# The first batch's keys of the first cross attention, made in the side attention's stage instead of ahead of the main attention

## The reference, cut to what matters

```python
y_dca = y[:, -DCA:, :]                    # the 16 side rows
y_main = y[:, :-DCA, :]                   # 1585 rows
kv_dca = (y_dca @ Wkv_dca + bkv_dca).reshape(b, DCA, 2, H, HD)
k_dca = _ln(kv_dca[:, :, 0], kn_dca_w, kn_dca_b)
v_dca = kv_dca[:, :, 1]
q = _ln((x @ Wq + bq).reshape(b, s1, H, HD), qn_w, qn_b)
kv = jnp.concatenate([y_main @ Wk + bk, y_main @ Wv + bv], axis=-1)
k = _ln(kv.reshape(b, s2, H, 2 * HD)[..., :HD], kn_w, kn_b)
ctx = _attn(qT, k.transpose(0, 2, 1, 3), v.transpose(0, 2, 1, 3))
ctx_dca = _attn(qT, k_dca.transpose(0, 2, 1, 3), v_dca.transpose(0, 2, 1, 3))
return (ctx + DCA_WEIGHT * ctx_dca) @ Wo + bo
```

## Time and profile before

| | us |
|---|---|
| median of 3 runs | 2436.7 |
| lowest, highest | 2436.36, 2438.23 |
| the profiled execution | 2434.61 |
| its span | 2432.8 |
| span to the first scores of the main attention | 120.72 |

### The profile page before, as it was taken

One profiled execution on the slowest core, in us unless ns is written; L12 is line 12 of the kernel. 1 busy time (PEld: TensorE's weight loads), 2 busy tenths in 40 slices (PEclk: granted clock), 3 DMA queues, 4 the chain that ended last, 5 costly groups with the idle time before them and its releaser, 6 DMA issues. The chain is left out here.

```text
span 2432.8 us, 47536 instructions
## 1 busy us (share of the span) xinstructions
PE 2227.4 (92%) x16972; PEld 1759.8 (72%) x16972; DVE 1589.0 (65%) x2655; ACT 1179.8 (48%) x2263; POOL 1031.2 (42%) x709
## 2 busy tenths in 40 slices
PE   4699999999998999979999999999999999788866
PEld 2677777777775888857777788888888887666644
DVE  5368877888787333334532788888888885566673
ACT  2355656665653333313213676676766673333241
POOL 5159888988895000001110455455455461111320
PEclk8699999999999999979999999999999999899989
DMA  3000000001001222114212000000000001211200
GB/s 117 0 28 28 29 29 2 29 29 42 10 2 37 66 69 69 39 24 100 69 66 66 28 28 10 21 28 18 12 28 28 1 27 44 67 40 44 87 1 18
DMA packets 106429, 89.92 MB, mean 37 GB/s; under 512 B 33105, under 2 KB 86625, under 8 KB 106225
## 3 DMA queue, kind: packets, MB, share of 16 engines
q1 hardware_dynamic: 105936, 87.21, 12.0%
q0 software_dynamic: 288, 0.00, 0.0%
HBM read 86.15 MB, written 1.05 MB: 36 GB/s over the span
## 5 line engine op out<-in xcount | busy, mean ns | idle before, releaser
L2508 POOL TENSOR_TENSOR xT<-xT,x1b_ring 128x512 f32<-128x512 f32 (+1 forms) x176 | 248.4, 1411 | 210.4 <-ACT x1b_ring L2665 203.5
L1096 POOL TENSOR_TENSOR x0b_krstd<-x0b_krstd,minus_half 128x24 f32<-128x24 f32 x64 | 266.8, 4169 | 85.9 <-DVE x0b_krstd L1163 83.1
L1116 POOL TENSOR_TENSOR xT<-xT,x0b_ring 128x512 f32<-128x512 f32 (+1 forms) x167 | 233.1, 1396 | 31.5 <-ACT x0b_ring L1351 15.6
L111 DVE TENSOR_TENSOR x1b_plo<-x1b_ring,x1b_phi 128x512 fp32r<-128x512 f32 (+1 forms) x208 | 224.1, 1078 | 6.0 <-issue 4.9
L1351 ACT ACTIVATE x0b_ring<-x0b_ring 128x512 f32<-128x512 f32 (+1 forms) x208 | 131.0, 631 | 168.3 <-DVE x0b_ring L1181 160.7
L2680 ACT ACTIVATE x1b_ring<-x_ps,x1b_keymask 128x512 f32<-128x512 f32 (+1 forms) x208 | 142.9, 687 | 130.3 <-DVE xT L2587 125.5
L116 PE MATMUL x_ps<-x1b_qy,x1b_yT 128*128 128x512 f32 (+1 forms) x416 | 175.1, 421 | 4.7 <-ACT x1b_ring L2680 3.3
L1194 DVE TENSOR_TENSOR x0b_ring<-x_ps,x0b_krstd 128x512 f32<-128x512 f32 (+1 forms) x208 | 142.6, 685 | 56.0 <-PE x_ps L956 54.0
L2587 DVE SCALAR_TENSOR_TENSOR xT<-x_ps,x1b_keymask,xT 128x512 f32<-128x512 f32 (+1 forms) x176 | 131.3, 746 | 57.6 <-PE x_ps L118 56.4
L116 PE MATMUL x_ps<-x1b_phi,x1b_yv 128*128 128x512 f32 (+1 forms) x416 | 166.3, 400 | 0.8 <-ACT x1b_out_sb L2647 0.8
L118 PE MATMUL x_ps<-x1b_qy,x1b_yT 128*128 128x512 f32 (+1 forms) x416 | 163.8, 394 | 0.0
(11 more groups left out here) (610 smaller groups left out, 5665.6 us busy)
## 6 DMA issues: line engine op xcount, KB each, us to landing
x_y<-in_ctx_dram SPq DMA_DIRECT2D x8, 1536.0 KB
x_y<-in_ctx_dram SPq DMA_DIRECT2D x24, 512.0 KB, 3.9
a_wn<-in_L_attn_W_Q_dram SPq DMA_DIRECT2D x16, 256.0 KB, 3.1
a_wn<-in_L_attn_W_K_dram SPq DMA_DIRECT2D x16, 256.0 KB, 3.6
a_wn<-in_L_attn_W_V_dram SPq DMA_DIRECT2D x16, 256.0 KB, 4.3
a_won<-in_L_attn_W_O_dram SPq DMA_DIRECT2D x16, 256.0 KB, 2.9
x1a_wq<-in_L_xattn_Wq_dram SPq DMA_DIRECT2D x8, 512.0 KB, 9.0
x_y<-in_L_xattn_Wo_dram SPq DMA_DIRECT2D x8, 512.0 KB, 3.6
```

The lines of the kernel that those rows point to most:

```text
L111: return v.tensor_tensor(lo, exact, hi.bitcast(F32), ALU.subtract)
L1096: ins = g_.tensor_tensor(r, r, c.minus_half[:, 0:8].unsqueeze(1).broadcast_to([P, whole, 8]), ALU.pow)
L1116: g_.tensor_tensor(total[half][0:m, :], old, src, ALU.add).then_inc(summed, 1)
L2508: g_.tensor_tensor(total[half][0:m, :], old, src, ALU.add).then_inc(summed, 1)
```

## The change

What the preparation and the 19 opening entries of the first batch need (tiles, semaphores, the entry code, the lists HERE and AHEAD) is now a class `Keys` in the outer stage, and all of it runs in x0a. There the entries have two PSUM banks, 4 and 5; the side attention's scores move to banks 2 and 3, and the side values are projected into bank 6 behind the last transposes of the heads. A list `PLAN`, read by all four engines, lays the groups' steps (S scores, F probabilities, O outputs) among the entries (X, so many of the list). The placing of the side values on ACT is split in four, one quarter behind each exponential, and PE waits for it in front of the first O rather than of the first S. The first queries are placed at the very end of x0a's ACT stream. In x0b the main attention begins with step 0. The steps and their entries are unchanged.

```diff
+class Keys:
+    OPEN_BANKS = (4, 5)
+    def put(self, name, banks):
+        bank = banks[self.number % len(banks)]
+        self.place[name] = bank, self.uses[bank]
+        self.uses[bank] += 1
+        self.number += 1
...
+    def make(self, pe, seq, e):
+        bank, nth = self.place[seq, e]
+        out = self.ps[:, bank, :]
+        pe.wait_ge(self.kv_free[bank], nth + 1)
...
+        PLAN = [("S", 0), ("X", 2), ("S", 1), ("F", 0), ("S", 2), ("X", 1), ("F", 1), ("S", 3), ("X", 1), ("F", 2), ("O", 0),
+                ("X", 2), ("F", 3), ("O", 1), ("X", 4), ("O", 2), ("O", 3), ("X", 9)]
...
             @block.vector
+                v.wait_ge(loaded_m, 24 * 16)
+                keys.vector_zero(v)
                 v.wait_ge(wv_done, 4)
...
-                for g in range(0, HG0, 2):
-                    for u in range(2):
-                        sm.vector_before_exp(v, ps[:, 4 + u, :], u, g + u)
-                    for u in range(2):
-                        sm.vector_after_exp(v, u, g + u)
+                for op, k in plan():
+                    if op == "S":
+                        sm.vector_before_exp(v, ps[:, 2 + k % 2, :], k % 2, k)
+                    if op == "F":
+                        sm.vector_after_exp(v, k % 2, k)
+                    if op == "X":
+                        keys.vector_take(v, 0, k)
...
             @block.tensor
+                def project_side_values():
+                    pe.wait_ge(bank_read, 3)
...
                 pe.wait_ge(scaled, T + 4)
-                pe.wait_ge(vs_done, 16)
-                scores(0)
-                scores(1)
...
+                keys.prepare(pe)
+                for op, k in plan():
+                    if op == "S":
+                        scores(k)
+                    if op == "F":
+                        flip(k)
+                    if op == "O":
+                        values(k)
+                    if op == "X":
+                        if k[0] == "K":
+                            pe.wait_ge(wkv_done, CC)
+                        keys.make(pe, 0, k)
...
             @block.scalar
+                for op, k in plan():
+                    if op == "S":
+                        sm.scalar_exp(act, k % 2, k)
+                        keep_side_values(k)
+                    if op == "F":
+                        tail(k)
+                    if op == "O":
+                        evacuate(k)
+                    if op == "X":
+                        keys.scalar_take(act, 0, k)
+                keys.place_queries(act, 0, 0)
...
-                steps(lambda e: make(0, e), step)
+                steps(step)
```

More of the change, by code:

```diff
@@ L525, in _ @@
                                       ).then_inc(wv_done, 1)
+                for op, k in plan():
+                    if op == "X" and k[0] == "T":
+                        keys.deviations(g, 0, k[1], k[2])
             @block.vector
@@ L643, in _ @@
                     flip_heads(j)
+                project_side_values()
                 def scores(g):
@@ L709, in _, with keep_side_values @@
                 act.wait_ge(vs_ready, 1)
-                for t in range(T):
+                def keep_side_values(t):
                     for j in range(4):
@@ L778, in x0_main_attention @@
         S_BANKS, O_BANK, M_BANK, KV_BANKS = (0, 1, 2), 3, 4, (5, 6, 7)
-        size = lambda kt: P if kt < FULL else TAIL0
+        size = keys.size
         four = lambda ap: ap.rearrange("p (t n) -> p t n", t=4)
-        def entries(text):
-            out = {}
-            for word in text.split():
-                n, what = word.split(":")
-                out.setdefault(int(n), []).append((what[0], *(int(x, 16) for x in what[1:])))
-            return out
-        HERE = entries("0:K030 0:T02 1:K031 2:W03 3:T03 3:K100 4:K101 5:W10 5:V0 6:T10 6:K110 6:V1 7:K111 7:V2 8:W11 8:V3 "
-                       "9:T11 9:K120 9:V4 10:K121 11:W12 11:V5 12:T12 12:V6 13:K130 14:K131 14:V7 15:W13 15:V8 16:T13 "
-                       "18:V9 20:Va 21:Vb 23:Vc")
-        AHEAD = entries("12:Y00 13:Y01 15:Y10 16:K000 16:Y11 17:K001 18:W00 19:T00 19:K010 20:K011 21:W01 22:T01 22:Y20 "
-                        "22:Y21 23:K020 24:K021 24:Y30 24:Y31 25:W02")
-        def made_at(part, n):
-            ahead = [] if part == "last" else AHEAD.get(n, [])
-            return [(0, e) for e in HERE.get(n, [])] + [(1, e) for e in ahead]
-        BEFORE = [e for n in sorted(AHEAD) for e in AHEAD[n]]
-        place, uses = {}, [0] * 8
-        def put(name):
-            bank = KV_BANKS[sum(uses) % len(KV_BANKS)]
-            place[name] = bank, uses[bank]
-            uses[bank] += 1
-        for e in BEFORE:
-            put((0, e))
+        def made_at(part, n):
+            ahead = [] if part == "last" else keys.AHEAD.get(n, [])
+            return [(0, e) for e in keys.HERE.get(n, [])] + [(1, e) for e in ahead]
+        place, kv_full, kv_free = keys.place, keys.kv_full, keys.kv_free
+        put = lambda name: keys.put(name, KV_BANKS)
         for seq in range(B):
@@ L850, in x0_main_attention @@
         late_done, late_inverted, late_normed = st.sem("late_done"), st.sem("late_inverted"), st.sem("late_normed")
[L851 to L856 removed]
+        projected, biased, ones_made = st.sem("projected"), st.sem("biased"), st.sem("ones_made")
+        apart = keys.apart
         def slot_of(seq, t):
@@ L863, in out_bank, with steps @@
             return S_BANKS[(TILES * B - len(S_BANKS) + t) % len(S_BANKS)] if t < T - 1 else place["rest"][0]
-        def steps(before, step):
-            for e in BEFORE:
-                before(e)
+        def steps(step):
             for seq in range(B):
@@ L1118, in step @@
                         if e[0] == "T":
-                            deviations(seq + ahead, e[1], e[2])
-                steps(lambda e: deviations(0, e[1], e[2]) if e[0] == "T" else None, step)
+                            keys.deviations(g_, seq + ahead, e[1], e[2])
+                steps(step)
                 g_.wait_ge(wo_loaded, 32)
@@ L1247, in step @@
                         v.tensor_tensor(o, osb[:, :, :], o, ALU.add).then_inc(added, 1)
-                steps(lambda e: take(0, e), step)
+                steps(step)
                 def add_output(t):
@@ L1319, in _ @@
-                ins.then_inc(prepared, 1)
-                act.wait_ge(prepared, 2)
-                def place_queries(seq, half):
-                    for j in range(4):
-                        rows = slice(32 * j, 32 * j + 32)
-                        act.activation(qbd[rows, 2 * half:2 * half + 2, S * j:S * j + S],
-                                       qT[rows, 2 * half:2 * half + 2, seq * S:seq * S + S], ACT.Identity,
-                                       scale=kn[rows, 0:1]).then_inc(q_placed, 1)
@@ L1352, in step @@
                     for ahead, e in made_at(part, n):
-                        take(seq + ahead, e)
-                steps(lambda e: take(0, e), step)
+                        keys.scalar_take(act, seq + ahead, e)
+                steps(step)
 HA, HDA = 16, 128
```

465 lines of the change are left out of this document (252 added, 213 removed).

## The result

The changed kernel took 2441.98 us (median of 8 runs, 2433.73 to 2445.27) beside 2436.62 for the kernel before (8 runs, 2429.29 to 2438.23): a ratio of 1.0021, 95% interval 1.0012 to 1.0030. The forecast was 2432.1. So the change, meant to start the main attention earlier, made the kernel slower, by 5.4 and 1.6 us in the two pairs of medians.

What follows compares the result with a forecast made beforehand. No single engine was taken to bound the opening, but a circular chain of waits; PE bounds the main attention. First scores at 114.8 plus 1.3 us slow clock gain 4.6: 2436.7 - 4.6 = 2432.1 us, range 2428.0 to 2437.0.

Steps and rivals of the forecast that it cites:

- The steps behind it are unchanged and gain or lose nothing: Main attention's steps after its start: no gain or loss, so the earlier effective start reaches the end.
- 4.6 was forecast: Whole kernel: gain in us from an effective main-attention start at 116.1 instead of 120.72.
- Steps (1) to (7): Walk through the opening to the main attention's first scores: 122.9 us at half clock, 104.8 at full, 114.8 taken.
- The four intervals of the probabilities: Steps (2) to (5), up to each group's probabilities on PE: 12.0, 10.0, 6.8, 7.3 us at half clock.
- The end of the preparation: Step (1), PE's side values and key preparation after the heads' transposes: ends at 61.0 us at half clock, 55.5 at full.
- the stretch from the last probabilities to the end of the deviations: Step (6), last outputs and entries up to W02: 23.3 us at half clock, 15.9 at full.
- 55% was forecast: Share of PE's opening work done at half clock, placing first scores at 114.8 us; 69% before the change.
- two rounds in one: Side attention and opening entries interleaved, so that one's waits may hold the other's work; entries took 27.6 us before.
- The start's clock: Main attention's first steps, behind 2.5 us of idle PE: 1.3 us lost to slow clock, bounds 0 and 3.4.
- Nothing of before shows its first steps at half clock: Main attention's start in the kernel before: clock 1.00, with no half-clock first steps seen.
- Rival C: Slower: serial chain at half clock throughout, effective start 126.3 us, 5.6 us late, time 2442; chance 0.05.
- Rival D: Start moves as forecast but a later stage waits for something else, time 2436.7; chance 0.05.

Runs made afterwards that it cites:

- e5_restore: Changed kernel with its ACT, PE and DVE instruction counts ahead of the main attention restored to match the kernel before: 2432.07 us, ratio 0.9979.
- e17_restore_again: Second timing of the changed kernel with all three instruction counts restored: 2434.50 us, ratio 0.9988 against the kernel before.
- the other rotation: Changed kernel with counts restored and its three PSUM banks' rotation begun as in the kernel before: 2434.47 us, ratio 0.9990.
- the gap: Changed kernel with counts restored and 2144 bytes left free ahead of the values and the ring: 2431.65 us, ratio 0.9982.
- e4_pad: Kernel before with six more ACT instructions at the side attention's end, to start the main attention later: 2438.14 us, ratio 1.0007.
- e15_dve128: Kernel before with 128 more increments on DVE ahead of the main attention: 2443.90 us in its one run.
- e12_place: Kernel before with the main attention's SBUF tiles in the changed kernel's order, instructions unchanged: 2436.84 us in its one run.

## Why the prediction was wrong

The step that failed is the sentence "The steps behind it are unchanged and gain or lose nothing". They are unchanged, but they do not stand where they stood. With 5, 5 and 1 more instructions ahead of them, the engines' pauses fall on other steps, and DVE's on the chain at 317, 583, 740 and 1041 us. That one instruction costs 5.65 us by itself (2443.20 against 2437.55; by the ratio's interval 3.9 to 9.3), more than the 4.1 us that the change typically had won at 130 us. Without it the changed kernel is at par with before (0.9998). With all three counts restored it is ahead in four timings, by 5.3 and 3.1 us (e5_restore, e17_restore_again), 2.0 with the other rotation and 5.9 with the gap; 4.6 was forecast.

The counts are not all of it. With them restored, main is still 1.5 to 2.9 us longer than before, from the drift and the meetings near 530 and 740 us, where the changed kernel's is 3.4 and 6.0 us longer.

- Steps (1) to (7): the sum was right, first scores forecast at 114.8, measured at 115.15. The four intervals of the probabilities came out as by half clock (12.0, 10.0, 6.8, 7.3 forecast; 12.2, from 57.70 to 69.91, then 10.1, 6.7 and 6.9 measured). The end of the preparation (57.8 between 55.5 and 61.0) and the stretch from the last probabilities to the end of the deviations (19.1 us between 15.9 and 23.3) lay between the two clocks. From 46 to 115.1 us 28.6 of the 41.9 busy us of PE ran at half clock, which is 52% of the work; 55% was forecast.
- The source of the earlier start: I put it down to two rounds in one. The order without overlap started as early (114.77, where the same walk gave 119 to 124). So the interleaving as such gave nothing that one profile of each could show, and part of the walk's agreement is luck.
- The start's clock: forecast 1.3 us, measured 2.6 against the one trace of before, and 2.0 to 2.6 in all profiles with the changed order. "Nothing of before shows its first steps at half clock" held for that trace alone; most later traces of kernels that start as before did lose 1.5 us there. The lead of 4.1 us between the means is near the 4.6 of the forecast.
- Rival C (slower) had a time of 2442, and 2441.98 was measured. That is luck: its mechanism was a start 5.6 us late, and the start was 5.6 us early.
- Rival D (the start moves, the time does not) came nearest in form, with a chance of 0.05, but it too named a later stage that waits for something else. I argued against it with the 95% busy PE, which speaks for a start carried through (e4_pad and e15_dve128 show it to 0.1 us up to 776 us), and did not ask whether the same instructions still take the same time.
- What the profile could have told: before's DVE addition at 582.62 led POOL's by 0.10 us, and its running maximum at 738.75 by 0.03. A stage with such margins can change its length when one engine shifts by a tenth of a microsecond.

Shown: the count on DVE causes the losses at 317, 583 and 1041 us and, in the kernel before with one increment, 1.3 us at 740; the count on ACT causes that at 168; 128 on DVE change nothing at these places (one profile); and the placement makes most of the drift (one profile). Argued only: that the pause is a wait for the block to be loaded, from the packets' times and the period; and that the granted clock's fall around 1041 us follows from the pause. Open: why the tiles' places make operations slower by some ns; what the 0.8 to 1.3 us near 740 in the restored kernels needs to go; the stretch from 776 to 1030 us, which took 258.6 to 262.0 us in the 18 profiles; and the stretch behind 1090 us, which took 1324.4 to 1335.4 us in them, with no relation to the kernel that I could find. Because of that spread a lead of 1 to 2 us at 756 us can't be followed to the medians one by one.

## What to carry to other kernels

Compare two versions of a kernel not only by the stage that was changed: count the instructions of each engine ahead of the long stages, waits and increments too, since one semaphore instruction moved this kernel by 5.65 us. Where a change is better by its own stage and worse by the clock, follow the lead along the trace by one engine's instructions counted from the end; it shows at once where it is lost. Then pad or trim the counts before judging the change (here 128 more on DVE left the places of its pauses as they were), and try a few offsets of the version that is kept. Take a second profile of the unchanged kernel too: here its lead at 130 us moved by 1.75 us with no change at all.

## What the runs showed of the hardware

- One more instruction on DVE ahead of a stage moved pauses of 0.35 to 0.4 us onto other steps (0.54 us instead of 0.15 ahead of one maximum, 0.51 instead of 0.16 ahead of one addition), and 128 more left them where they were. On ACT, 5 more put a gap of 0.41 us between two instructions, and 5 + 123 more took the loss there away.
- A DVE addition of 128x128 with two SBUF inputs took 0.29 us at 583 us, and 1.16 us when a POOL addition had begun 0.26 us before it. A maximum of 128x512 took 0.69, and 1.70 and 1.88 with a POOL power beside it; but one took 0.69 in the middle of a POOL power of 4.17 us. At 740 us starts 0.03 us apart went with 0.69 or 1.88.
- Moving tiles in SBUF, with the same instructions, made the main attention 0.58 us longer, in steps of 0.02 to 0.06 us about every 20 us (e12_place, one profile).
- 18 profiled executions that share the same instructions behind 1090 us took from 1324.4 to 1335.4 us for them. The first steps of the main attention, unchanged, took 1.5 us more in some executions than in others, with a stretch of half clock there.
